# Order of loads, halos and stores on the sync engine's queue in a fused four-block convolution network

## The reference

```python
x = x + _L0_conv_ref(_gn(x), L0_conv_W, L0_conv_b)
x = x + _L1_conv_ref(_gn(x), L1_conv_weight)
x = x + _L2_conv_ref(_gn(x), L2_conv_base_weight, L2_conv_spline_weight, L2_conv_spline_scaler, L2_conv_bias_weight)
x = x + _L3_conv_ref(_gn(x), L3_conv_combinator, L3_conv_bias)
```

## Time and profile before

| what | us |
|---|---|
| median of 3 runs | 1353.57 (1351.46 to 1354.47) |
| the profiled execution | 1358.18 |
| its span, first to last instruction | 1356.4 |
| PE busy | 1188.7 |
| DVE busy | 770.5 |
| ACT busy | 700.4 |
| POOL busy | 505.8 |

### The profile page before, as it was taken

The page is one execution under the profiler, slowest core; times in us unless marked ns, Lnnn a source line. Parts: engine busy times, 40 slices in busy tenths (PEclk is TensorE's granted clock), DMA queues, the critical chain, the costliest instruction groups (busy, mean ns, idle before and its releaser), DMA issues.

```text
span 1356.4 us, 14842 instructions
## 1 busy us (share of the span) xinstructions
PE 1188.7 (88%) x5088; PEld 882.0 (65%) x5088; DVE 770.5 (57%) x946; ACT 700.4 (52%) x740; POOL 505.8 (37%) x810
## 2 busy tenths in 40 slices
PE   1289999999999999999999999999965568888884
PEld 0265677766666677766666677777744446766663
DVE  5489972465565422364646512566434498988732
ACT  2377864453444434444435434433323698988721
POOL 5654655443512043423133147764632231000002
PEclk9999999999999999999999999999977878888888
DMA  9599989999999686999999788886632144466564
GB/s 90 141 265 245 273 262 277 217 216 189 198 191 224 172 206 189 244 192 199 187 191 229 173 251 238 235 228 176 141 62 47 26 74 69 78 98 97 95 98 62
DMA packets 107215, 232.12 MB, mean 171 GB/s; under 512 B 41332, under 2 KB 55236, under 8 KB 98948
## 3 DMA queue, kind: packets, MB, share of 16 engines
q1 hardware_dynamic: 73888, 131.34, 48.4%
q0 software_dynamic: 32704, 99.57, 27.3%
q10 hardware_dynamic: 548, 0.27, 0.2%
HBM read 122.05 MB, written 85.75 MB: 153 GB/s over the span
## 4 chain that ended last, share of the span: by engine, by line
PE 63%; DVE 11%; SPq 9%; DMA 5%; ACT 5%; issue 4%; POOL 3%; DVEq 0%; ACTq 0%; POOLq 0%
PE PB L1646 51%; PE PB L1617 10%; SPq L750 7%; DVE F L1400 2%; DMA S<-lattice 2%; DVE F L1388 2%; DVE F L1474 1%; ACT F L1088 1%; SPq L736 1%; SPq L778 1%; ACT F L1198 1%; POOL taps L834 1%; PE PB L1608 1%; DMA S<-in_x 1%; DMA lattice<-S 1%
## 5 line engine op out<-in xcount | busy, mean ns | idle before, releaser
L1646 PE MATMUL PB<-F,WA 128*96 128x512 f32 (+1 forms) x3792 | 916.9, 403 | 35.7 <-DVE F L1400 25.3
L1646 PEld LDWEIGHTS PB<-F,WA 128*96 128x96 f32 (+1 forms) x3792 | 661.4, 175 | 281.9 <-issue 39.1
L1099 ACT ACTIVATE S<-PB,BIAS 96x512 f32<-96x512 f32 (+1 forms) x320 | 211.7, 682 | 314.7 <-PE PB L1646 314.2
L1088 ACT ACTIVATE F<-S 128x2116 fp32r<-128x2116 f32 (+4 forms) x160 | 261.2, 1633 | 199.8 <-DMA S<-lattice 164.0
L994 POOL DMA_DIRECT2D lattice<-S x240 | 130.7, 554 | 515.1 <-ACT S L1099 496.6
L1388 DVE TENSOR_TENSOR F<-S,F 128x1089 fp32r<-128x1089 f32 (+2 forms) x80 | 121.4, 1518 | 214.8 <-ACT F L1088 214.3
L1617 PE MATMUL PB<-F,WA 128*128 128x512 f32 x576 | 159.4, 440 | 36.2 <-DVE F L1474 36.2
L1400 DVE CAST F<-F 64x528 fp32r<-64x528 f32 (+4 forms) x304 | 186.3, 662 | 3.5
L1390 DVE TENSOR_TENSOR F<-S,F 128x1058 fp32r<-128x1058 f32 x64 | 80.7, 1262 | 184.1 <-ACT F L1088 183.3
L1617 PEld LDWEIGHTS PB<-F,WA 128*128 128x128 f32 x576 | 122.2, 214 | 68.6 <-issue 37.7
L809 POOL TENSOR_TENSOR RS<-VE,NHALF 128x1 f32<-128x1 f32 (+1 forms) x25 | 19.7, 787 | 170.7 <-DVE VE L1313 170.6
(11 more groups left out here) (124 smaller groups left out, 778.9 us busy)
## 6 DMA issues: line engine op xcount, KB each, us to landing
lattice<-S POOLq DMA_DIRECT2D x48, 817.5 KB, 7.0
S<-lattice SPq DMA_DIRECT2D x448, 66.1 KB, 5.5
lattice<-S POOLq DMA_DIRECT2D x96, 272.5 KB, 4.5
S<-lattice SPq DMA_DIRECT2D x160, 136.1 KB, 2.7
S<-lattice SPq DMA_DIRECT2D x72, 272.5 KB, 5.3
S<-lattice SPq DMA_DIRECT2D x160, 70.1 KB, 2.7
S<-lattice SPq DMA_DIRECT2D x80, 136.2 KB, 5.4
S<-lattice SPq DMA_DIRECT2D x160, 66.0 KB, 3.0
```

Source lines behind the costliest of these rows:

```text
L1088: act.activation(piece_view(s, h, 0), raw_view(s, h), ACT.Copy).then_inc(hi_ready, 1)
L1099: act.activation(wide(to[:, at:at + TS])[:, :, 0:RX], pixels(RING_BANK[n % SLOTS_O][0:cell.rows, :]), ACT.Relu, bias=BIAS[0:cell.rows, k:k ...
L1646: last = nc.tensor.matmul(bank, WA[0:rows, first:first + cell.rows], wide(FZ[0:rows, i % SLOTS_F, base:base + TS])[:, :, 0:RX], start=j == ...
```

## The change

Three parts of the order are changed; the arithmetic stays as it is.

- **Stores.** SP issues the lattice's stores (`store_outputs`), each four steps late: behind the loads of step s come the stores of step s-4, ahead of them a wait for that step's evacuation. POOL still waits for each evacuation but issues none of them. POOL's stores of the first block's input count on semaphores of their own, `input_stored`.
- **Last cell.** SP issues all loads of cell 15 and then the circular halos of images 0 to 7. PE makes `l1_step(b - 4)` behind cell step b, DVE and POOL take the updates, norms and tails of block 1 one image later, and one more circular step, with its update and tail, stands behind the last cell. `EVENTS` is numbered to match.
- **Final convolution.** In a KAN image PE makes `l3_step(b - 3)` behind SiLU, ahead of group 1, instead of at the end. SP issues `l3_halos(b - 3)` ahead of the waits and copies of group 0, instead of behind them.

```diff
--- before.py
+++ after.py
@@ -42,6 +42,7 @@
 SLOTS_F = 3
 SLOTS_S = 3
 SLOTS_O = 4
+STORE_LAG = 4
 SLOTS_1 = 3
 SSLOT = 2 * SEG + 1
 TOP = 1 + EVEN
@@ -176,7 +177,7 @@
     TPK = nc.dram_tensor("taps_kan", (2, 2, KC, FEATS * 4 * C), F32, kind="Internal").ap()
 
 
-    pieces_before, chunks_before, stores_before = [0], [0], [4]
+    pieces_before, chunks_before, stores_before = [0], [0], [0]
     for cell in cells:
         stores_before.append(stores_before[-1] + cell.stores)
         for b in range(B):
@@ -221,7 +222,7 @@
     EVENTS = []
     for i in range(B + 5):
         EVENTS += [(0, i)] if i < B else []
-        EVENTS += [(1, i - 4)] if 0 <= i - 4 < B else []
+        EVENTS += [(1, i - 5)] if 0 <= i - 5 < B else []
     EVENTS += [(2, b) for b in range(B)]
     EVENT_AT = {event: n + 2 for n, event in enumerate(EVENTS)}
 
@@ -357,6 +358,7 @@
         l3_clear = sem("l3_clear")
 
         image_stored = [sem(f"image_stored{b}") for b in range(B)]
+        input_stored = [sem(f"input_stored{b}") for b in range(B)]
         image_loaded = [sem(f"image_loaded{q}") for q in range(SLOTS_K)]
         tp_stored = sem("tp_stored")
         w_loaded = [sem("w_loaded0"), sem("w_loaded1")]
@@ -735,6 +737,13 @@
                 for dst, src in image_halos(F1[:, z, :, 0:TS], F1[:, z, :, TS:2 * TS], True):
                     sp.dma_start(dst, src).then_inc(l1_halo[z], 16)
 
+            def store_outputs(s):
+
+                if s // B < NC - 1:
+                    sp.wait_ge(evac_done, chunks_before[s + 1])
+                    for dst, src in output_stores(s):
+                        sp.dma_start(dst, src).then_inc(image_stored[s % B], 16)
+
             for s in range(STEPS):
                 k, b = divmod(s, B)
                 q, before = halves_before[s] % SLOTS_K, last_user[s]
@@ -745,15 +754,18 @@
 
                 if s == 4 * B:
                     sp.wait_ge(kr_clear, 4)
-                sp.wait_ge(image_stored[b], 16 * stores_before[k])
+                if k == 0:
+                    sp.wait_ge(input_stored[b], 4 * 16)
+                else:
+                    sp.wait_ge(image_stored[b], 16 * stores_before[k])
                 for dst, src in input_loads(s):
                     sp.dma_start(dst, src).then_inc(image_loaded[q], 16)
+                if s >= STORE_LAG:
+                    store_outputs(s - STORE_LAG)
                 if (k, b) in RAW_STEPS:
                     sp.wait_ge(turned, TURN_AT[f"cell{RAW_STEPS[k, b] - 2}"])
                     load_taps(RAW_STEPS[k, b])
-                if k == NC - 1 and b >= 4:
-                    l1_halos(b - 4)
-            for j in range(4, B):
+            for j in range(B):
                 l1_halos(j)
 
             def l3_halos(b):
@@ -764,6 +776,9 @@
                     sp.dma_start(dst, src).then_inc(l3_halo[max(0, b - B + 3)], 16)
 
             for b in range(B):
+                if b >= 3:
+                    sp.wait_ge(l3_clear, 1)
+                    l3_halos(b - 3)
                 for g in range(KAN_SETS):
                     if b:
                         sp.wait_ge(tile_used, used(b - 1, f"halo{g}"))
@@ -776,9 +791,6 @@
                     sp.wait_ge(feat_lo, KAN_SETS * b + g + 1)
                     for dst, src in group_halos(g):
                         sp.dma_start(dst, src).then_inc(halo_rows[g], 16)
-                    if g == 0 and b >= 3:
-                        sp.wait_ge(l3_clear, 1)
-                        l3_halos(b - 3)
             l3_halos(B - 3)
             sp.wait_ge(l3_clear, 2)
             l3_halos(B - 2)
@@ -934,7 +946,7 @@
             for b in range(B):
                 pool.wait_ge(xn_ready, b + 1)
                 for dst, src in image_store(None, b, XS[:, b % 3]):
-                    pool.dma_start(dst, src).then_inc(image_stored[b], 16)
+                    pool.dma_start(dst, src).then_inc(input_stored[b], 16)
             for s in range(STEPS):
                 k, b = divmod(s, B)
 
@@ -944,7 +956,7 @@
                     clear_taps(TURN_STEPS[k, b])
                 if k == 5 and b == 0:
                     for image in range(B):
-                        pool.wait_ge(image_stored[image], 4 * 16)
+                        pool.wait_ge(input_stored[image], 4 * 16)
                     load_kan(range(4))
                 if k == 5 and b == 1:
                     load_kan(range(4, 8))
@@ -990,14 +1002,13 @@
                     store_taps(TURN_STEPS[k, b - 2])
                 if k < NC - 1:
                     pool.wait_ge(evac_done, chunks_before[s + 1])
-                    for dst, src in output_stores(s):
-                        pool.dma_start(dst, src).then_inc(image_stored[b], 16)
                 else:
                     if b >= 1:
                         norm_event(0, b - 1)
-                    if b >= 5:
-                        norm_event(1, b - 5)
+                    if b >= 6:
+                        norm_event(1, b - 6)
             norm_event(0, B - 1)
+            norm_event(1, 2)
             norm_event(1, 3)
             pool.wait_ge(out_done, TOTCH)
             pool.memset(L3S[0][:, 1].bitcast(F32), 0.0).then_inc(l3_clear, 1)
@@ -1129,7 +1140,7 @@
             for b in range(B):
                 act.wait_ge(norm_ready, 1)
                 if b >= 3:
-                    act.wait_ge(image_stored[b - 3], 4 * 16)
+                    act.wait_ge(input_stored[b - 3], 4 * 16)
                 normalise(wide(XS[:, b % 3, 1:1 + TS])[:, :, 0:RX], pixels(X[:, b]), b).then_inc(xn_ready, 1)
             act.wait_ge(bias_ready, 1)
             for i in range(2):
@@ -1430,14 +1441,15 @@
                                             wide(staged(s)[:, 1:1 + TS])[:, :, 0:RX], ALU.add).then_inc(added[0], 1)
                     dve.wait_ge(added[0], b + 1)
                     image_stats(0, b)
-                    if b >= 4:
-                        l1_update(b - 4)
+                    if b >= 5:
+                        l1_update(b - 5)
                     if b >= 1:
                         tail(0, b - 1)
                     if b >= 2:
                         l1_split_lo(b - 2)
-                    if b >= 5:
-                        tail(1, b - 5)
+                    if b >= 6:
+                        tail(1, b - 6)
+
             def update(b):
 
                 dve.wait_ge(tile_used, used(b, "halo1"))
@@ -1506,11 +1518,13 @@
 
             tail(0, B - 1)
             l1_split_lo(B - 2)
+            l1_update(3)
+            tail(1, 2)
             l1_update(4)
-            tail(1, 3)
             inner(0)
             l1_split_lo(B - 1)
             outer(0)
+            tail(1, 3)
             l1_update(5)
             basis(0)
             tail(1, 4)
@@ -1688,11 +1702,13 @@
                         pe.wait_ge(bias_ready, 1)
                     if b >= 1:
                         group_means(0, b - 1)
-                    if b >= 3:
-                        l1_step(b - 3)
-                    if b >= 5:
-                        group_means(1, b - 5)
+                    if b >= 4:
+                        l1_step(b - 4)
+                    if b >= 6:
+                        group_means(1, b - 6)
             group_means(0, B - 1)
+            l1_step(B - 4)
+            group_means(1, 2)
             l1_step(B - 3)
             group_means(1, 3)
             l1_step(B - 2)
@@ -1758,10 +1774,10 @@
                         pe.wait_ge(silu_lo, b + 1)
                         todo = [(own_weights(BASES, dx), at_shift(feature(BASES), P, dx)) for dx in range(2)]
                         products(bank, todo, False, False).then_inc(tile_used, 1)
+                        if b >= 3:
+                            l3_step(b - 3)
                 if b == 0:
                     group_means(1, 6)
-                if b >= 3:
-                    l3_step(b - 3)
             group_means(2, B - 2)
             halo_steps(B - 1, 0)
             halo_steps(B - 1, 1)
```

## The result

The changed kernel took 1319.47 us in the median of 4 runs (1315.63 to 1321.44), the kernel before 1352.51 beside it: a ratio of 0.9758, 95% interval 0.9722 to 0.9793. The forecast was 1306, with a range of 1293 to 1331. So the gain was 33 us where 48 was forecast.

A forecast was written before the change was run, and what follows sets the result against it. It took PE's 168 us idleness as winnable, from in-order waits through SP and ACT, no engine being full in KAN images. Terms -32.4-20.0-1.5+6 = -47.9 us gave 1310.3, or 1306 on the medians' scale; own range 1298 to 1315, 8-in-10 range 1293 to 1331.

The forecast's parts named there:

- Part 1: Last cell: loads ahead of halos and the circular step later start kan_image(0) earlier, -32.4 us; bound -26.7.
- halo 0: Last cell: the first circular halo goes out at 993.75 us as now, with circular step 0 starting at 1002.3.
- The one wait of PE: Last cell: PE idles about 4 us once before circular steps, and little more until kan_image(0).
- Part 2: KAN images: final convolution inside the image removes ACT's wait at L1210; 25.6 us an image, -20.0 us in all.
- Rival B: KAN images: halo copies become the next loop, 28 us an image, part 2 gives 10 us, 1316 us; chance 0.13.
- Tail: Last KAN image: SP's 2.8 us of halo issues no longer precede the last group's copies; -1.5 us.
- Part 3: Lattice: stores issued by SP four steps late cost +6 us, between -6 and +25.
- The bound of +25: Lattice: upper price of SP's stores, 0.8 us in each of 32 three-input steps.
- still keeps up: Three-input cells: SP waits 1.6 us a step; one more issue leaves 1.1, so its queue suffices.
- Theory L: From the experiments: late stores hold ACT's staging slots; lag 5 slower by 6 us or far more.
- Rival C: Lattice gains because SP's stores go out sooner than POOL's: -6 us instead of +6, 1294 us; chance 0.07.
- rivals A: Three-input steps: SP's one queue starves PE, 0.8 us a step, 26 us instead of 6, 1326 us; chance 0.17.

The follow-up runs named there:

- experiment 4: The kernel before with only the final convolution moved inside the KAN image and its halos ahead of group 0: 1328.35 us, ratio 0.9817 to the kernel before.
- experiment 1: The changed kernel with the lattice's stores issued by POOL again and none by SP: 1292.36 us, ratio 0.9552 to the kernel before.
- experiment 3: The kernel before with SP issuing all last-cell loads ahead of the circular halos, circular step still at b - 3: 1330.18 us, ratio 0.9826.
- experiment 7: The changed kernel with POOL issuing all stores and SP only waiting for the evacuation of step s-4: 1295.32 us, ratio 0.9570 to the kernel before.
- experiment 5: The changed kernel with SP storing only cells 0 to 4 and POOL storing cells 5 to 14: 1319.83 us, ratio 0.9756 to the kernel before.
- experiment 8: The changed kernel with stores on POOL; SP keeps its waits and issues a 64-byte DMA per store: 1406.82 us, ratio 1.0379 to the kernel before.
- experiment 11: The changed kernel with stores on POOL; SP issues a 64-byte DMA per store, without evacuation waits: 1390.80 us, ratio 1.0262 to the kernel before.
- lag 5: The changed kernel with each store five steps late instead of four: 1628.33 us, ratio 1.2035 to the kernel before.

## Why the prediction was right in direction and 13 us too low

**Part 1, right.** -32.4 forecast, -33.4 in the trace, -36 between medians (experiments 4 and 1). Where it came from was half right: loads ahead give 19 to 23, the step later 11 to 15 (experiment 3), and the prediction told the stall by the first of these alone. One detail failed: halo 0 went out 19.2 us after the last cell's start instead of 17.9, since SP came late out of the lattice and ACT had waited 2.57 us for a load. The one wait of PE was 2.65 us, not 4.

**Part 2, right.** -20.0 forecast, -21.2 in the trace. The period is 25.3 us, ACT's 25.1 as read from rows 9. Rival B (halo copies) did not come.

**Tail, right in sign, too small.** -1.5 forecast, -5.4 measured: the sum counted SP's 2.8 us ahead of the last halos, and left out that in the last image too the first 42 matmuls get faster when the gap ahead of them shrinks (10.22 against 12.73 us).

**Part 3 is the failed term.** +6 forecast, +21.5 in the trace against before, +27 in medians against experiment 1. The step that failed is "Between 60 and 330 SP waits 36.3 us, and 69 stores want 38", and with it the price of 2 us beyond SP's waits. The window ended at 330, inside cell 5, and the 14.5 us behind L1391 belong to the three-input steps of cell 5, where slack is of no use to cells 0 to 4. Those five cells alone have 13.5 + 8.3 = 21.8 us of SP's waits, against 8 x (2+1+1+2+2) = 64 stores, 35 us at 0.55. By that the shortage was 13 us at the least, not 2. And a queue doesn't use up all its waits: 11.7 us were left, so that 35 - (21.8 - 11.7) = 25 us should remain; 21.2 were measured. The forecast of about 4 us where the short steps hand over to 16 loads a step had the right place and half the size: PE's gap there is 7.93 us. The bound of +25 held the 21.5 of the traces, though not the 27 of the medians, and that by luck: it was placed in 32 three-input steps, which lost nothing. That SP "still keeps up" there was right.

What bounds cells 0 to 4 by this reading is SP's queue: issues in 195.8 of 214.9 us, ACT's splits starting as loads land, the loads' landing no slower, no price of the order wait that shows (experiment 7), the same stores from POOL free (1), and the price in the early cells alone (5). Experiments 8 and 11, meant to show the queue time by itself, couldn't, so that the size of the term rests on these, not on an isolated dose. Theory L applies at lag 5 and not at lag 4: in the changed kernel ACT waits for stores in the three-input cells without delaying PE.

The Trainium skill, "DMA: Bandwidth & Descriptors", section "Issuing engines are not separate DMA queues", says that a second issuing engine saves only sequencer time, "usually small relative to the DMA itself". The trace fits the first half in the main: from SP the stores land 1 us sooner, no more (817.5 KB in 6.0 us between 60 and 330, 7.0 from POOL). The second is so for one issue (0.58 us beside 4.2 to landing, medians of SP's stores between 54 and 345), but doesn't help here, where the queue is the bound of five cells. Rival C, for which the prediction cites the Trainium skill, "SBUF — State Buffer", section "SBUF: two separate sides" (some VectorE instructions hold up the descriptors of DMAs issued by GpSimd), found no support: with POOL issuing, the lattice was the shortest of all, 913.4 and 914.3 us (experiments 7 and 1).

Put together: 1306 + 21 (stores, 27 instead of 6) - 4 (tail) - 1 (part 2) - 1 (part 1) = 1321, against 1319.5. With the 21.5 of the two traces in the place of the 27, it would be 1315.5, near the profiled execution's 1315.63.

The time lies in the range for 8 in 10 (1293 to 1331), but outside the forecast's own range (1298 to 1315). By the terms named for it, stores at 0 or 12 and part 1 at its bound, that range should have been 1300 to 1318, and 1319.5 lies outside this too. The upper part of the wide range was there for rivals A and B, and neither came: that it held the time is in part luck.

## What to carry to other kernels

Before a DMA issue is moved to another queue, count that queue's issues against its step in each kind of step by itself, with the window cut where the kind changes; slack of a neighbouring kind is not slack. A place in an in-order queue is a lag with two cliffs: too soon, and the wait holds back the loads (+46 to 49 us), too late, and what it feeds starves (+309 us). A bundle of edits with a net gain can hide a loss: undoing the stores gave 27 us more.

## What was unexpected of the hardware

- DMAs of 64 bytes from DRAM to DRAM, 88 in 176 us, raised the DMA engines' share from 0.78 to 1.02 and the landing of 70 KB stores from 2.7 to 6.8 us. That they move next to nothing doesn't make them free.
- An issue's time doesn't follow its bytes. The tiny DMAs had the longer median on SP (min, median, max ns) than the lattice's stores:

```profile
L754 SPq DMA_DIRECT2D tiny<-in_L_conv_bias x240: 493/589/2926, 62.2 to 1087.1; - x120
```

```profile
L745 SPq DMA_DIRECT2D lattice<-S x240: 303/452/1712, 59.7 to 994.9; - x120
```
